# Per-head dt, running sums and decays in two 128-row tiles, turned by two transposes a step; one turn and two ScalarE copies reordered

## What is computed

```python
proj = layernorm(x) @ W_in * mup_vector           # 512 -> z 1024 | x 1024, B 128, C 128 | dt 64
xBC = silu(conv_b + causal 4-tap conv of xBC)
dt = softplus(dt + dt_bias)                       # per token and head, 64 heads of 16 channels
dA = exp(dt * -exp(A_log))
state = state * dA + (dt * x_t) outer B_t;  y_t = state . C_t       # over the tokens
g = (y + D * x) * silu(z);  g = g * rsqrt(mean(g^2) + eps) * norm_w
x = x + g @ W_out
x = x + (silu(gate(n)) * up(n)) @ down.T * down_s,  n = layernorm(x)
```

## Time and profile before

| | us |
|---|---|
| median of the timed runs | 771.53 (771.21 to 771.61, 3 runs) |
| the profiled execution, whole | 765.49 |
| its span | 763.8 |
| TensorE busy in the span | 731.8 |
| VectorE, ScalarE, GpSimd busy | 518.0, 492.3, 294.5 |
| mixer, up to the MLP's first product | about 509 |

### The profile page before, as it was taken

One profiled execution on the slowest core, in us unless ns is written; L12 is line 12 of the kernel. 1 busy time (PEld: TensorE's weight loads), 2 busy tenths in 40 slices (PEclk: granted clock), 3 DMA queues, 4 the chain that ended last, 5 costly groups with the idle time before them and its releaser, 6 DMA issues.

```text
span 763.8 us, 20312 instructions
## 1 busy us (share of the span) xinstructions
PE 731.8 (96%) x8486; PEld 606.8 (79%) x8486; DVE 518.0 (68%) x845; ACT 492.3 (64%) x933; POOL 294.5 (39%) x235
## 2 busy tenths in 40 slices
PE   4976999999999999999999999989999999999997
PEld 4865888888887887887888887778888888888886
DVE  5968976987997797797797798864524433532331
ACT  5989978978978978979879888723313312321320
POOL 2074376467457537628618708720021011002002
PEclk9989999999999999999999999999999999999999
DMA  9833144484495275366276279735022013002002
GB/s 294 237 75 112 44 103 118 86 256 129 84 241 145 81 211 163 92 152 201 78 226 190 71 220 310 231 115 157 23 70 97 1 53 112 0 27 83 0 1 85
DMA packets 42299, 94.97 MB, mean 124 GB/s; under 512 B 9888, under 2 KB 15776, under 8 KB 42016
## 3 DMA queue, kind: packets, MB, share of 16 engines
q1 hardware_dynamic: 42208, 93.67, 42.4%
HBM read 84.73 MB, written 17.57 MB: 134 GB/s over the span
## 4 chain that ended last, share of the span: by engine, by line
PE 82%; DVE 7%; ACT 7%; issue 2%; POOL 1%; DMA 1%; SPq 0%; ACTq 0%; DVEq 0%; POOLq 0%
PE ps_y L1692 10%; PE ps_proj L1679 10%; PE ps_proj L1225 8%; PE ps_proj L1226 7%; PE ps_proj L1227 7%; PE ps_out L1679 6%; PE ps_x L1679 6%; PE ps_y L1301 5%; PE ps_out L1325 3%; PE ps_x L1312 3%; PE ps_x L1278 3%; PE ps_out L1326 3%; PE ps_out L1327 3%; ACT ring L717 1%; DVE cx L938 1%
## 5 line engine op out<-in xcount | busy, mean ns | idle before, releaser
L532 POOL TENSOR_TENSOR ring<-tokd,ring 128x1024 f32<-128x1024 f32 x64 | 123.0, 1936 | 175.1 <-ACT tokd L712 127.6
L1225 PE MATMUL ps_proj<-xn_hi,win_x_hi 128*128 128x256 f32 x352 | 103.8, 295 | 2.3 <-DVE xn_lo L907 2.3
L1226 PE MATMUL ps_proj<-xn_lo,win_x_hi 128*128 128x256 f32 x352 | 99.5, 283 | 0.0
L1227 PE MATMUL ps_proj<-xn_hi,win_x_lo 128*128 128x256 f32 x352 | 99.2, 282 | 0.0
L938 DVE SCALAR_TENSOR_TENSOR cx<-cin,consts,cx 128x256 f32<-128x256 f32 x240 | 96.3, 478 | 0.0
L1548 POOL TENSOR_TENSOR res<-res,hidden 128x512 f32<-128x512 f32 (+1 forms) x16 | 20.1, 1257 | 166.3 <-DVE hidden L1611 160.6
L993 DVE TENSOR_TENSOR ring<-ring,ps_tok 128x1024 f32<-128x1024 f32 x64 | 75.6, 1214 | 7.1 <-ACT ring L721 7.0
L1225 PEld LDWEIGHTS ps_proj<-xn_hi,win_x_hi 128*128 128x128 f32 x352 | 66.9, 190 | 15.6 <-issue 8.2
L1225 PE MATMUL ps_proj<-xn_hi,win_z_hi 128*128 128x256 f32 x256 | 73.9, 289 | 0.0
L1226 PE MATMUL ps_proj<-xn_lo,win_z_hi 128*128 128x256 f32 x256 | 72.3, 282 | 0.0
L1227 PE MATMUL ps_proj<-xn_hi,win_z_lo 128*128 128x256 f32 x256 | 72.1, 282 | 0.0
(11 more groups left out here) (186 smaller groups left out, 1882.0 us busy)
## 6 DMA issues: line engine op xcount, KB each, us to landing
ring<-cum_dram SPq DMA_DIRECT2D x128, 256.0 KB, 4.9
xin<-x SPq DMA_DIRECT2D x8, 512.0 KB, 4.3
res<-x SPq DMA_DIRECT2D x32, 128.0 KB, 2.7
x_dram<-res SPq DMA_DIRECT2D x32, 128.0 KB, 2.4
res<-x_dram SPq DMA_DIRECT2D x16, 256.0 KB, 2.6
out<-res SPq DMA_DIRECT2D x15, 256.0 KB, 2.1
x_in_sb<-x_dram SPq DMA_DIRECT2D x3, 1024.0 KB, 5.9
gate_w_copy<-gate_w SPq DMA_DIRECT2D x4, 704.0 KB, 6.5
```

Source lines behind the costliest of these rows:

```text
L532: pool.tensor_tensor(ring[:, g, :, :], own, ring[:, g, :, :], ALU.subtract).then_inc(diffed, 1)
L1225: pe.matmul(out, hi[:, k, :], xn_hi[:, k, :], start=(k == 0), stop=False)
L1226: pe.matmul(out, hi[:, k, :], xn_lo[:, k, :], start=False, stop=False)
L1227: made = pe.matmul(out, lo[:, k, :], xn_hi[:, k, :], start=False, stop=(k == KT - 1))
```

## The change

dt and cum move into one tile `dt_cum`, dt on rows 0 to 63 (heads) and cum on rows 64 to 127, with (step, sequence, token) along the row, 256 in all; run and to_end likewise into `run_end`. So a step's part of each tile is 128x128, and turn_tokd makes two transposes in place of eight 64x64 products. make_dt becomes two operations (one for each sequence), to_end four; d is made in cum's place and the scan runs in place, over 256 along the row on 64 rows. The wait for the last block's store of cum moves from make_cum to make_d, and ScalarE's wait for cum_made ahead of dt_p goes. step_decay becomes [64, 2, 2]. In the orders, TensorE's turn_tokd(i, 1) goes behind project(i, 9), ScalarE's keep_tokd(i, 1) behind evacuate 9, and keep_tok(c) of a first step ahead of square and evacuate 7. low_row becomes a part of low_buf.

```diff
         self.low_buf = sb(ctx, "low_buf", [P, LOW_WIDTHS[2]])
-        self.low_row, self.low_any = sb(ctx, "low_row", [1, P]), sb(ctx, "low_any", [1, 1])
+        self.low_row, self.low_any = self.low_buf[0:1, 0:P], sb(ctx, "low_any", [1, 1])
         self.stats, self.moments = sb(ctx, "stats2", [P, TT, 6]), sb(ctx, "moments2", [P, TT, 2])
...
         dt_v, dt_e, dt_p = sb("dt_v", [P, P]), sb("dt_e", [P, P]), sb("dt_p", [P, P])
-        dts = sb("dts", [P, 4, P])
+        dt_cum, run_end = sb("dt_cum", [P, STEPS, BATCH, Q]), sb("run_end", [P, STEPS, BATCH, Q])
+        UPPER, LOWER = slice(0, HEADS), slice(HEADS, P)
         tok = sb("tok", [P, P])
         tokd = sb("tokd", [P, STEPS, 4, HEADS])
-        whole, step_decay = sb("whole", [P, BATCH * HEADS, STEPS]), sb("step_decay", [P, STEPS])
+        whole, step_decay = sb("whole", [P, BATCH * HEADS, STEPS]), sb("step_decay", [HEADS, BATCH, STEPS])
         consts = sb("consts", [P, C_N])
...
         causal = sb("causal", [P, Q])
-        chain = sb("chain", [P, P])
+        chain = sb("chain", [P, STEPS * BATCH * Q])
...
                 for j in range(STEPS):
-                    sp.dma_start(cum_dram[bass.ds(i, 1), j, :, :].rearrange("a r t -> (a r) t"),
-                                 dts[:, CUM, half(j)]).then_inc(cum_out, 16)
+                    sp.dma_start(cum_dram[i, j, :, :].rearrange("(b h) t -> h b t", b=BATCH),
+                                 dt_cum[LOWER, j, :, :]).then_inc(cum_out, 16)
...
                 sp.wait_ge(step_decayed, i + 1)
-                sp.dma_start(whole_dram[bass.ds(i, 1), :, :].rearrange("a r j -> r (a j)"), step_decay[:]).then_inc(whole_out, 16)
+                sp.dma_start(whole_dram[i, :, :].rearrange("(b h) j -> h b j", b=BATCH), step_decay[:]).then_inc(whole_out, 16)
...
             sp.wait_ge(hand.low_all_made, 1)
-            sp.dma_start(hand.low_row[:], hand.low_all[:]).then_inc(hand.low_in, 16)
+            sp.dma_start(hand.low_row, hand.low_all[:]).then_inc(hand.low_in, 16)
             sp.dma_start(hand.scales[:], mlp_packed).then_inc(hand.scales_in, 16)
...
                     act.wait_ge(dt_exp, j + 1)
-                    act.wait_ge(cum_made, j)
                     act.activation(dt_p[:], dt_e[:], ACT.Copy, scale=log_c[-1]).then_inc(soft_step, 1)
...
                 act.wait_ge(whole_out, 16 * i)
-                act.activation(step_decay[:], dts[:, CUM, Q - 1::Q], ACT.Exp).then_inc(step_decayed, 1)
+                act.activation(step_decay[:].rearrange("h b j -> h j b"), dt_cum[LOWER, :, :, Q - 1], ACT.Exp).then_inc(step_decayed, 1)
                 act.wait_ge(tokd_turned, STEPS * i)
-                act.activation(dts[:, RUN, :], dts[:, CUM, :], ACT.Exp).then_inc(run_made, 1)
+                act.activation(run_end[UPPER, :, :, :], dt_cum[LOWER, :, :, :], ACT.Exp).then_inc(run_made, 1)
                 for j in range(STEPS):
-                    at = (j + 1) * Q - 1
-                    made = act.activation(dts[:, TO_END, half(j)], dts[:, CUM, half(j)], ACT.Exp, scale=-1.0,
-                                          bias=dts[:, CUM, at:at + 1])
+                    for b in range(BATCH):
+                        made = act.activation(run_end[LOWER, j, b, :], dt_cum[LOWER, j, b, :], ACT.Exp, scale=-1.0,
+                                              bias=dt_cum[LOWER, j, b, Q - 1:Q])
                 made.then_inc(to_end_made, 1)
...
                 clamp(c, 1)
+                keep_tok(c)
                 if not first:
...
                     evacuate(i, 7)
-                keep_tok(c)
                 fade(c, 0)
...
                 evacuate(i, 8)
+                evacuate(i, 9)
                 keep_tokd(i, 1)
-                evacuate(i, 9)
                 if first:
...
+            def by_step(t, r):
+
+                return t[r, :].rearrange("p (j t) -> p j t", j=STEPS)
+
             def make_dt(j, opening=False):
...
                     dve.wait_ge(tokd_turned, STEPS * j)
-                dve.tensor_tensor(dts[:, DT, :], dt_v[:], dt_p[:], ALU.add).then_inc(dt_made, 1)
-
-            def make_d(j):
+                for b in range(BATCH):
+                    r = slice(b * HEADS, (b + 1) * HEADS)
+                    made = dve.tensor_tensor(dt_cum[UPPER, :, b, :], by_step(dt_v, r), by_step(dt_p, r), ALU.add)
+                made.then_inc(dt_made, 1)
+
+            def make_d(j, opening=False):
                 dve.wait_ge(dt_made, j + 1)
-                dve.tensor_scalar(dt_p[:], dts[:, DT, :], neg_a[:], LOWEST, ALU.mult, ALU.max).then_inc(d_made, 1)
-
-            def make_cum(j, opening=False):
-                dve.wait_ge(d_made, j + 1)
                 if not opening:
                     dve.wait_ge(cum_out, 32 * j)
-                dve.tensor_tensor_scan(dts[:, CUM, :], chain[:], dt_p[:], 0.0, ALU.mult, ALU.add).then_inc(cum_made, 1)
+                dve.tensor_scalar(dt_cum[LOWER, :, :, :], dt_cum[UPPER, :, :, :], neg_a[UPPER, :], LOWEST, ALU.mult, ALU.max).then_inc(d_made, 1)
+
+            def make_cum(j):
+                dve.wait_ge(d_made, j + 1)
+                cums = dt_cum[LOWER, :, :, :].rearrange("p j b t -> p (j b t)")
+                dve.tensor_tensor_scan(cums, chain[LOWER, :], cums, 0.0, ALU.mult, ALU.add).then_inc(cum_made, 1)
...
                 dve.wait_ge(hand.low_in, 16)
-                dve.tensor_reduce(hand.low_any[:], hand.low_row[:], mybir.AxisListType.X, ALU.max,
+                dve.tensor_reduce(hand.low_any[:], hand.low_row, mybir.AxisListType.X, ALU.max,
                                   apply_absolute_value=True).then_inc(hand.low_any_made, 1)
...
             dve.wait_ge(a_negated, 1)
-            make_d(0)
+            make_d(0, opening=True)
             dve.wait_ge(filled, 2)
-            make_cum(0, opening=True)
+            make_cum(0)
             conv_taps(0, CONV_ORDER[0:2])
...
                     pe.wait_ge(gvar_made, c - 1)
-                for n in range(4):
-                    for b in range(BATCH):
-                        made = pe.matmul(ps_tokd[half(b), n * HEADS:(n + 1) * HEADS], dts[half(b), n, half(j)], eye[half(b), half(b)],
-                                         start=True, stop=True)
+                for n, pair in enumerate((dt_cum, run_end)):
+                    made = pe.transpose(ps_tokd[:, n * P:(n + 1) * P], pair[:, j, :, :].rearrange("p b t -> p (b t)"), eye[:])
                 made.then_inc(tokd_turned, 1)
...
                 update(c, 0)
-                turn_tokd(i, 1)
                 if first:
...
                 project(i, 9)
+                turn_tokd(i, 1)
                 group(c, 2)
...
```

## The result

The changed kernel takes **774.61 us** in the median (769.18 to 777.97), the kernel before beside it on the same chip 771.48 (767.82 to 775.06), 14 runs each; the ratio is 1.0042, 95% interval 1.0022 to 1.0061. Run again later it gave 1.0070 (1.0044 to 1.0096). So it is slower, by 0.4 to 0.7%, 3 to 5 us. I had forecast 768.6 and a range of 764.8 to 771.5: wrong in sign, and outside the range. The profiled execution of the kernel after took 774.51 us, span 772.7, at a mean granted clock of 0.985; the one of before had a span of 763.8 at 0.995.

A forecast was written before the change was run, and what follows sets the result against it. TensorE, busy 96%, was taken to bound the kernel, with VectorE's and ScalarE's path 0.91 us behind and then setting blocks 1 to 6. Gains of 1.85 + 0.85 + 0.23 = 2.9 us off 771.53 gave 768.6, range 764.8 to 771.5.

The forecast's parts named there:

- the opening and block 0: Up to block 0's carry: 1.6 us gained from a vanished collision, less 0.57 and 0.2, net 0.85 us less.
- Term 1: TensorE's turns: two 128x128 transposes for eight 64x64 products save 0.41 us a turn, 0.82 a block.
- Term 2: VectorE's longer make_dt, make_d and scan add 0.57 us a block, between 0.3 and 0.75.
- The sum for blocks 1 to 6: VectorE's and ScalarE's path, 46.38 us from carry to second update, sets the pace: 0.28 us gained a block, 1.85 over six.
- The moves: Second turn and its copy behind projection 9, keep_tok sooner: avoid waits in each block, costed at nothing.
- Term 3: ScalarE's longer run and four to_end operations add 0.6 us a block, covered by VectorE's taps in blocks 1 to 7.
- The opening's collision: Block 0's normalise against GpSimd's first difference: it goes, normalise takes 1.0 us for 2.63, 1.6 us less.
- 0.2 taken off: Block 0: 0.2 us deducted because the next VectorE operations may meet GpSimd's difference for longer.
- Block 7: Carry's scaled rows ready 0.85 us ahead; 0.41 off and 0.63 on leave 0.23 us gained.
- Rival D: Slower, chance 0.10: normalise's second operation meets GpSimd's first difference in every block, 6.7 us lost, 778.2 us.

The follow-up runs named there:

- VectorE short: Kernel after with VectorE's dt, d and running sum cut to the old amount, leaving out some sums, ScalarE in full: 769.83 us, ratio 1.0016.
- The moves alone: Kernel before with only the later turn_tokd and its copy and the sooner keep_tok, old tile layout: 768.39 us, ratio 0.9981.
- the stream shifted: Kernel after with TensorE instructions added: 256 waits 1.0116, 256 waits for a semaphore met earlier 1.0135, 80 instructions in block 0's idle times 1.0034.

## Why the prediction was wrong, step by step

Three steps failed. In the opening and block 0 the forecast had 0.85 us gained up to the carry, and they were lost instead: 1.5 us by the first traces, 2.0 to 2.2 counted from TensorE's first product. Each of blocks 1 to 6 gained 0.1 us for 0.28. And the sum put at nothing, without a reason, that another program has its instruction packets elsewhere: between block 0 and 1 the traces have a gap with a lower clock behind it, 4.9 and 6.7 us more than before, and in the last groups another. The sum itself has a slip of no weight: five times 0.28 and 0.38 are 1.78, not 1.85.

**Term 1 was right.** The turns take 0.50 us a block for 1.22, 0.72 saved for 0.82 forecast; with VectorE short the period falls by 0.70.

**Term 2 was too small**, 0.72 us for 0.57 (inside my ends of 0.3 and 0.75): the scan was right, the serial step from the second dt operation to d was missing.

**The sum for blocks 1 to 6** had the right mechanism and the wrong place. I took the second update as the place where VectorE is late. It is late sooner, at the carry addition: the rows end 0.85 us ahead of it before, a number that I used for block 7 alone. Less 0.41 for the turn and 0.63 for VectorE (in block 4 the rows end 37.88 us after the carry with the additions, 37.25 without) it is 0.2 late, plus the release; 0.35 was measured, six times. The gain is 0.1 us a block instead of 0.28, so about 1.2 us of the forecast's 1.85 never came. TensorE's 0.70 and VectorE's 0.60 (59.60 for 59.00) cancel.

**The moves were right**, but not at nothing: without them the block would be 60.0 us, and in block 7 sum_squares waits for the kept tokd, 0.23 to 0.72 us in the kernels with both parts (the 0.2 us to spare that I named).

**Term 3 was right for blocks 1 to 6** (59.00 against 59.09) **and too small in the opening.** Timeline of ScalarE in the opening, before and then after:
```profile
24.48 0.29 ACT L672 ACTIVATE dts<-dts 128x128 f32<-128x128 f32 x1
24.68 0.57 ACT L675 ACTIVATE dts<-dts 128x64 f32<-128x64 f32 x2
```
```profile
24.54 0.40 ACT L672 ACTIVATE run_end<-dt_cum 64x256 f32<-64x256 f32 x1
24.96 1.05 ACT L675 ACTIVATE run_end<-dt_cum 64x64 f32<-64x64 f32 x4
```
From the start of run to the end of to_end it is 26.01 - 24.54 = 1.47 us for 25.25 - 24.48 = 0.77, 0.70 more, and nothing is in front of ScalarE to take that up: it copies tokd 0.9 us later (33.57 for 32.66). TensorE's first product came 0.56 sooner in that trace (8.35 for 8.91); counted from it, run begins 0.62 later and the copy 1.47. So VectorE's 0.6 and ScalarE's 0.7 lie one behind the other here. ScalarE has no gap behind the copy, turn_x waits for its cx, and xpad comes 1.5 us later by the same count (42.20 for 41.26). The forecast had taken 0.57 for both together, from the first difference, which by this count is indeed only 0.55 later (37.49 for 37.50).

**The opening's collision did not go, it moved.** This is the term of 1.6 us. Timeline of VectorE in block 0, before (the earlier trace rows has the normalise ahead of them), then after:
```profile
57.16 3.05 DVE L885 SCALAR_TENSOR_TENSOR wout_lo<-rows,consts,wout_hi 128x512 fp32r<-128x512 f32 x2
...
61.27 1.40 DVE L885 SCALAR_TENSOR_TENSOR wout_lo<-skip,consts,wout_hi 128x512 fp32r<-128x512 f32 x2
```
```profile
56.03 1.00 DVE L901 TENSOR_SCALAR xin<-xin,moments,rstd 128x512 f32<-128x512 f32 x2 [1.12 <-POOL rstd L512]
56.95 1.41 DVE L885 SCALAR_TENSOR_TENSOR wout_lo<-rows,consts,wout_hi 128x512 fp32r<-128x512 f32 x2
58.27 1.22 DVE L1008 COPY state<-ps_x 128x1024 f32<-128x1024 f32 x1
59.53 3.65 DVE L885 SCALAR_TENSOR_TENSOR wout_lo<-skip,consts,wout_hi 128x512 fp32r<-128x512 f32 x2
63.11 1.28 DVE L907 TENSOR_TENSOR xn_lo<-ps_proj,xn_hi 128x512 fp32r<-128x512 f32 x2
...
66.76 3.05 DVE L885 SCALAR_TENSOR_TENSOR wout_lo<-res,consts,wout_hi 128x512 fp32r<-128x512 f32 x2
```
Normalise takes 1.00 us now, the weight pair behind it 1.41 for 3.05, and the state copy is done 1.86 us sooner, all as forecast. But GpSimd's differences have to be made all the same. They start 3.4 us later (58.43 for 55.05) and now lie on the next weight pairs, 3.65 for 1.40 us and 3.05, and xn_lo stands behind the first of these. That is the 3.0 us in which TensorE waits for xn_lo. My "0.2 taken off" for this was 2.25 in the first pair alone. For TensorE little changed: before, it waited 3.32 us for the state copy behind the slow pair and 0.60 for xn_lo, 3.9 in all; after, 0.4 and 2.98, 3.4 in all. The moves alone, with the old tiles, give the same picture:
```profile
60.53 3.65 DVE L885 SCALAR_TENSOR_TENSOR wout_lo<-skip,consts,wout_hi 128x512 fp32r<-128x512 f32 x2 [0.68 <-ACT wout_hi L629]
...
65.43 0.39 PE L1225 MATMUL ps_proj<-xn_hi,win_x_hi 128*128 128x256 f32 x1 [3.03 <-DVE xn_lo L907]
```
So it is the later copy of tokd that moves the collision. Behind the wait the clock was at 1.2 GHz from 64.0 to 67.4 us, with products of 256 columns 0.21 us apart for 0.12, and again for 3.4 us from 77.6, behind the wait for xpad. The second trace of the kernel after has both (64.3 and 77.9), the two of the kernel before have the first at most (60.2). That in block 0 no order escapes the collision, and only less work on VectorE or GpSimd would, is my reading; it was not tried.

**Block 7** and the end: last carry to the end of the program 277.7 us for 276.2, with a gap of 2.5 us in the last groups, beside a packet, and the lower clock for 3.4 us behind it; the 0.23 us of gain can't be seen. Up to the mixer's last product it is 3.5 and 2.0 us more than before (24.66 and 24.18 for 21.20 and 22.16). How much of it is work and how much packets I can't tell apart.

**What no rival had** is the largest item in the traces. With the stream shifted, the stretch from block 0's carry to block 1's takes 60.09 to 60.12 us in three kernels, for 66.84 and 65.03 unshifted: 4.9 to 6.7 us for the gap and the clock behind it. The medians show less of it, as a gap comes elsewhere in each: 1.0039 (the waits taken off) and 1.0034 (with 1.3 us of waits still in it) for 1.0070 and 1.0042, which is up to 2.5 us and not clear of the intervals. What is left, 0.2 to 0.4%, fits the opening (1.5 to 2.2 us up to the carry of block 0) and an unknown part of the last groups, less 0.6 of blocks 1 to 6. By this estimate the change as such lies between no difference and 3 us lost, and the rest of the 3 to 5 is the place of its packets; no run separates the two. The times of single edits, apart by less than some 3 us, can't be told from that; so the medians alone do not show that block 0's order is harmless or that ScalarE's part in block 0 is. Rival D ended on the right side for the wrong reason: normalise takes 1.0 us in every block after. Nor did I have a rival in which the change loses in block 0 what it gains elsewhere, and that was open to see: three engines are dense there, and 0.85 of my 2.9 us hung on one order of events among them.

## What to carry to other kernels

Find the slack of a path at each place where the other engine is waited for, not at the last one alone: here the room was 0.91 us at the second update and 0.85 at the carry addition, and the turn's own place had less still, and the smallest decides. Moving work past a contended stretch moves the contention unless the total falls. And in a long unrolled program a change of a few hundred instructions may move a 2 to 3 us stall in or out; here an edit of ScalarE's program alone did. Before a difference of 0.4% is put down to the work, compare two traces of each kernel stage by stage, look for gaps without a wait, and shift the stream once to see what is left.
